# Narrow attention scores in one pass over packed query parts, packed narrow outputs, and two sets of probabilities

## The reference

```python
# wide (layers 0, 2)
q, k, v = hidden @ Wq, ctx @ Wk, ctx @ Wv            # 16 heads of 64
logits = einsum('bhqd,bhkd->bhqk', q, k) * 64**-0.5 + col_bias
out = softmax(logits) @ v ;  out = out @ Wo + bo + residual
# narrow (layers 1, 3)
xn = rmsnorm(x, norm_w); q = xn @ wq                  # 16 heads of 16
k, v = cond @ wk, cond @ wv                           # 4 heads of 16
scores = einsum('btgrd,bsgd->bgrts', qg, k) * 0.25
out = softmax(scores) @ v ;  return residual + out @ wo
```

## Time and profile before

| | us |
|---|---|
| median of 3 runs | 1891.38 |
| lowest, highest | 1888.63, 1896.26 |
| profiled execution | 1886.37 |
| its span on the core | 1883.9 |
| TensorE busy | 1703.7 (90%) |
| VectorE busy | 1251.6 (66%) |
| ScalarE busy | 1040.1 (55%) |
| GpSimd busy | 428.8 (23%) |

### The profile page before, as it was taken

One profiled execution on the slowest core, in us unless ns is written; L12 is line 12 of the kernel. 1 busy time (PEld: TensorE's weight loads), 2 busy tenths in 40 slices (PEclk: granted clock), 3 DMA queues, 4 the chain that ended last, 5 costly groups with the idle time before them and its releaser, 6 DMA issues. The chain is left out here.

```text
span 1883.9 us, 29965 instructions
## 1 busy us (share of the span) xinstructions
PE 1703.7 (90%) x10924; PEld 935.7 (50%) x10924; DVE 1251.6 (66%) x2393; ACT 1040.1 (55%) x1761; POOL 428.8 (23%) x299
## 2 busy tenths in 40 slices
PE   6897597989999999999899999899999999999574
PEld 5786333444545454545445454445454545454333
DVE  4447554667867786878566777577777777776342
ACT  1111063666666666666566666566666666666231
POOL 4242302121222122212111322121212121312201
PEclk9998698999999999999999999999999999999786
DMA  8976542051215121513243324222332233221205
GB/s 270 326 266 207 130 125 47 13 102 35 75 44 124 35 75 44 124 36 95 69 100 76 88 49 101 58 70 60 83 65 71 60 82 66 70 60 50 56 25 201
DMA packets 176025, 175.78 MB, mean 93 GB/s; under 512 B 89538, under 2 KB 131902, under 8 KB 174281
## 3 DMA queue, kind: packets, MB, share of 16 engines
q1 hardware_dynamic: 173576, 163.39, 33.0%
q10 hardware_dynamic: 2304, 10.49, 1.4%
HBM read 127.17 MB, written 46.63 MB: 92 GB/s over the span
## 5 line engine op out<-in xcount | busy, mean ns | idle before, releaser
L1183 DVE TENSOR_REDUCE tops<-general 128x2 bf16<-128x308 f32 x1024 | 436.6, 472 | 105.3 <-PE general L1290 47.8
L1143 POOL TENSOR_TENSOR kept<-kept,inv_b 128x512 f32<-128x512 f32 x192 | 258.6, 1368 | 659.6 <-DMA inv_b<-scratch_inverses 655.3
L1046 ACT ACTIVATE probs<-score_ps 128x512 f32<-128x512 f32 x512 | 299.4, 597 | 137.9 <-PE score_ps L1326 130.4
L1170 DVE CAST q_aux<-q_pair 64x512 bf16<-64x512 f32 x160 | 82.7, 517 | 211.4 <-ACT q_pair L1034 210.3
L1056 ACT ACTIVATE q_aux<-general 4x512 bf16<-4x512 bf16 x320 | 187.6, 586 | 13.6 <-PE general L1297 6.7
L1033 ACT ACTIVATE q_pair<-general 64x512 fp32r<-64x512 f32 x160 | 94.6, 592 | 178.3 <-PE general L1271 178.0
L1082 ACT ACTIVATE a_hi<-kept 128x512 fp32r<-128x512 f32 x192 | 109.9, 621 | 122.3 <-POOL kept L1143 62.8
L1196 DVE TENSOR_TENSOR a_lo<-kept,a_hi 128x512 fp32r<-128x512 f32 x192 | 149.8, 821 | 28.6 <-ACT a_hi L1082 27.8
L1216 DVE TENSOR_TENSOR x<-general,x 128x512 f32<-128x512 f32 x160 | 108.4, 690 | 80.5 <-PE general L1384 79.2
L1286 PE MATMUL general<-w_top,q_aux 128*128 128x154 bf16 x1024 | 125.7, 234 | 24.0 <-DVE q_pair L1173 10.5
L1131 POOL TENSOR_TENSOR x_lo<-xn,x_hi 128x1024 fp32r<-128x1024 f32 x32 | 75.8, 2368 | 308.0 <-ACT x_hi L1014 157.1
(11 more groups left out here) (150 smaller groups left out, 3249.3 us busy)
## 6 DMA issues: line engine op xcount, KB each, us to landing
inv_b<-scratch_inverses SPq DMA_DIRECT2D x128, 256.0 KB
inv_b<-scratch_inverses SPq DMA_DIRECT2D x128, 128.0 KB
xn<-scratch_stream SPq DMA_DIRECT2D x16, 512.0 KB, 3.8
w_pair<-scratch_wk_hi SPq DMA_DIRECT2D x32, 256.0 KB
x<-scratch_stream SPq DMA_DIRECT2D x16, 512.0 KB, 3.3
scratch_stream<-x SPq DMA_DIRECT2D x16, 512.0 KB, 4.0
scratch_wk_hi<-p_kout_hi SPq DMA_DIRECT2D x16, 308.0 KB
p_raw<-in_L_xattn_Wk_dram SPq DMA_DIRECT2D x4, 1024.0 KB, 6.9
```

Source lines behind the costliest of these rows:

```text
L1046: nc.scalar.activation(dst, score_ps[:, number % 2, :], ACT.Exp, scale=scale).then_inc(act_exp.sem, 1)
L1143: last = nc.gpsimd.tensor_tensor(tile, tile, inv_b[:, i, :], ALU.mult)
L1183: last = nc.vector.tensor_reduce(tops[:, n % 2, sub, 2 * pair:2 * pair + 2], src, AX_X, ALU.max)
```

## The change

- **Narrow scores in one pass.** `q_pair` for narrow steps holds tiles of 32 rows (two heads of 16) in three bands: high part, low part, high part again, and four rows (96 to 99) of negated maxima. The keys `n_pair` lie against them as high, high, low keys, and ones for the maxima, all in fp32r. So a narrow score is one matmul, not two; `n_aux` is gone. A narrow `rest` is two fp32r matmuls over pairs of heads, where it was one fp32r and one bf16.
- To fill the bands: DVE casts the whole query bank to bf16 (`n_query`, for the maxima), ACT makes four copies of 32 rows, DVE four subtractions of 32 rows, POOL copies the high band (32 x 2048) to rows 64 to 95. A narrow `turn` writes two tiles instead of one.
- **Packed narrow outputs.** Values of odd key heads are laid in the other 16 rows of each 32. Two tiles are scaled by inverses that are zero on the rows of sums (`inv_n`, 16-row DMAs, eight a batch where four were) and POOL adds them into one. `norm`, `low` and `output` of a narrow batch then handle one tile and six matmuls, not two and twelve.
- **Two probability sets.** `probs` is doubled; the exponential waits for `value` two steps back.
- Inverses have one DRAM buffer and one spread buffer for each kind of layer, so `inverse c` waits for the scales of the chunk two back, not the one before. The `general` banks are counted over the whole plan. `ORDER` is a new one.

```diff
-        sums=d("sums", (H, TOK), F32), inverses=d("inverses", (H, TOK), F32),
+        sums=d("sums", (H, TOK), F32), inverses=d("inverses", (2, H, TOK), F32),
...
+        n_query = sb("n_query", [P, 2, TOK], BF16)
-        probs = sb("probs", [P, 4, TOK])
+        probs = sb("probs", [P, 2, 4, TOK])
...
# SP, inverses of a narrow chunk
+                        for j in range(4):
+                            at = 32 * j + DN * h
+                            src = rows[4 * j + 2 * batch + h:4 * j + 2 * batch + h + 1]
+                            sp.dma_start(inv_n[at:at + DN, h, :], src.to_broadcast([DN, TOK])).then_inc(inv_loaded[1].sem, 16)
...
# ACT
+                        wait(act, dve_aux.sem, dve_aux.after(it, what, n, k))
+                        for pair in range(4):
+                            last = nc.scalar.activation(q_pair[0:32, s, pair, :], ps[32 * pair:32 * pair + 32], ACT.Copy)
...
-                    before_w, before = back_step(it, n, 3 if what == "rest" else 1)
+                    before_w, before = back_step(it, n, 3 if what == "rest" else 2)
...
+                        for pair in range(2):
+                            last = nc.scalar.activation(q_pair[96:100, slot(n), 2 * (n % 2) + pair, :], tops_t, ACT.Copy, scale=-1.0)
...
-                    for i in range(2):
+                    for i in range(1 + (n + 1) % 2):
                         tile = chunk_tile(n, 2 * k + i)
                         last = nc.scalar.activation(a_hi[:, i, :], kept[:, place(tile), :], ACT.Copy)
...
# POOL
+                    wait(pool, act_query.sem, act_query.after(it, what, n, k))
+                    pool.wait_ge(*latest)
+                    q = q_pair[:, slot(n)]
+                    nc.gpsimd.tensor_copy(q[64:96], q[0:32]).then_inc(pool_query.sem, 1)
...
+                    if n % 2:
+                        last.then_inc(pool_parts.sem, 1)
+                        wait(pool, pool_parts.sem, pool_parts.after(it, "scale", n, k))
+                        last = nc.gpsimd.tensor_tensor(tiles[0], tiles[0], tiles[1], ALU.add)
...
# DVE
+                        wait(dve, pe_query.sem, pe_query.after(it, what, n, k))
+                        nc.vector.tensor_copy(n_query[:, s, :], ps).then_inc(dve_aux.sem, 1)
...
+                        for pair in range(4):
+                            last = nc.vector.tensor_tensor(q_pair[32:64, s, pair, :], ps[32 * pair:32 * pair + 32], q_pair[0:32, s, pair, :], ALU.subtract)
...
# PE
+                        if not wide(n):
+                            wait(pe, pool_query.sem, pool_query.after(it, *query_for(n, 1)))
...
-                        h, unit = 4 * g + k, k if wide(n) else n % 2
-                        if what == "rest":
-                            keys = (n_pair_rest[:, g], n_aux_rest[:, g])
-                        else:
-                            keys = (w_pair[:, h], w_aux[:, h]) if wide(n) else (n_pair[:, h], n_aux[:, h])
-                        nc.tensor.matmul(ps, keys[0], q_pair[:, s, unit, :], start=True, stop=False)
-                        last = nc.tensor.matmul(ps, keys[1], q_aux[:, t, s, unit, :], start=False, stop=True)
+                        last = nc.tensor.matmul(ps, n_pair[:, 4 * g + k], q_pair[:, s, 2 * (n % 2) + k // 2, :], start=True, stop=True)
...
-                        pairs = [q for i in range(2) for q in split3(w[0][:, 2 * k + i, rows], w[1][:, 2 * k + i, rows], a_hi[:, i, :], a_lo[:, i, :])]
+                        tiles = [(2 * k + i, i) for i in range(2)] if n % 2 == 0 else [(k, 0)]
+                        pairs = [q for at, i in tiles for q in split3(w[0][:, at, rows], w[1][:, at, rows], a_hi[:, i, :], a_lo[:, i, :])]
```

Of the new `ORDER`, the narrow steps 4 to 6, which the inverses and scales of chunk 0 run through:

```diff
+    rest 4, score 4 0, score 4 1, max 5 6, max 5 7, score 4 2, max 6 0, max 6 1, score 4 3, turn 5,
+        max 6 2, max 6 3, inverse 0, split 2, value 4 1, max 6 4, max 6 5,
+    rest 5, score 5 0, max 6 6, output 3- 1, score 5 1, max 6 7, score 5 2, max 7 0, max 7 1, score 5 3,
+        query 8 0, turn 6, value 5 1,
+    rest 6, max 7 2, max 7 3, score 6 0, scale 0 0, norm 0 0, max 7 4, max 7 5, scale 0 1, max 7 6,
+        scale 0 2, max 7 7, max 8 0, score 6 1, max 8 1, score 6 2, scale 0 3, max 8 2, turn 7, max 8 3,
+        score 6 3, low 0 0, query 8 1,
```

More of the change, by code:

```diff
@@ L558 @@
-    rest 15, value 14 1, score 15 0, output 2 0, wkeys 0+ 2, score 15 1, max 0+ 4, wkeys 0+ 3, score 15 2,
-        norm 2 1, max 0+ 5, max 0+ 6, score 15 3, max 0+ 7, low 2 1, query 1+ 0, turn 0+, value 15 1,
-        scale 2 2, output 2 1, norm 2 2, scale 2 3, max 1+ 0, low 2 2, query 1+ 1
+    rest 0, max 1 0, score 0 0, max 1 1, max 1 2, score 0 1, sums 3-, max 1 3, score 0 2, max 1 4,
+        max 1 5, value 0 0, scale 2- 2, max 1 6, norm 2- 2, score 0 3, scale 2- 3, inverse 3-, max 1 7,
+        scale 3- 0, low 2- 2, query 2 0, turn 1, value 0 1, output 2- 2, max 2 0, norm 2- 3,
@@ new lines @@
+    rest 10, max 11 0, max 11 1, max 11 2, value 9 0, max 11 3, scale 1 0, max 11 4, score 10 0, max 11 5,
+        score 10 1, max 11 6, max 11 7, score 10 2, score 10 3, turn 11, value 9 1, query 12 0, early 0+,
+    rest 11, max 12 0, value 10 0, scale 1 1, max 12 1, norm 1 0, score 11 0, value 10 1, max 12 2,
+        score 11 1, max 12 3, max 12 4, score 11 2, max 12 5, low 1 0, max 12 6, score 11 3, max 12 7,
+        query 14 0, turn 12, value 11 0, value 11 1, max 13 0, max 13 1, sums 2, max 13 2,
@@ new lines @@
+    rest 12, max 13 3, max 13 4, score 12 0, max 13 5, max 13 6, score 12 1, max 13 7, score 12 2,
+        output 1 0, turn 13, inverse 2, score 12 3, norm 1 1, max 14 0, max 14 1, max 14 2, max 14 3,
+    rest 13, split 0+, max 14 4, wkeys 0+ 0, max 14 5, score 13 0, low 1 1, max 14 6, score 13 1, max 14 7,
+        value 12 1, max 15 0, max 15 1, score 13 2, max 15 2, turn 14, output 1 1, score 13 3, max 15 3,
+    rest 14, max 15 4, scale 2 0, max 15 5, wkeys 0+ 1, score 14 0, norm 2 0, max 15 6, max 15 7,
+        score 14 1, low 2 0, query 0+ 0, wkeys 0+ 2, turn 15, query 0+ 1, wkeys 0+ 3, score 14 2,
+        value 13 1, score 14 3, output 2 0,
@@ L561 @@
+    rest 15, scale 2 1, max 0+ 0, score 15 0, max 0+ 1, max 0+ 2, score 15 1, norm 2 1, max 0+ 3, max 0+ 4,
+        value 14 1, max 0+ 5, max 0+ 6, score 15 2, max 0+ 7, low 2 1, score 15 3, query 1+ 0, turn 0+,
+        query 1+ 1, value 15 1, output 2 1
 """
@@ L575, in window @@
     return order
-WINDOW = window()
-ROUNDS = range(-1, ITER + 1)
+WINDOW = window(ORDER)
 def chunk_of(what, n):
@@ L620, in back_tile, with plan @@
     return w, tile
+def plan():
+    entries = []
+    for r in range(-1, ITER + 1):
+        entries += [(r + turn, what, n, k) for what, n, k, turn in WINDOW if present(r + turn, what, n)]
+    return entries
+PLAN = plan()
 class Signal:
```

302 lines of the change are left out of this document (145 added, 157 removed).

## The result

| | before | after |
|---|---|---|
| median | 1891.01 us (20 runs, 1885.62 to 1897.32) | 1899.08 us (20 runs, 1890.10 to 1907.92) |
| ratio, 95% interval | | 1.0041 (1.0025 to 1.0058) |
| span of the profiled execution | 1883.9 us | 1903.0 us |

The forecast was 1811 us; the change makes the kernel slower by 0.4%, some 8 us. The profiled execution of after took 1904.78 us, 5.7 above its median, so its spans overstate the loss.

A forecast was written before the change was run, and what follows sets the result against it. TensorE's work was taken as the bound. Scores -56, rest +2, outputs -45, probabilities -4, new waits +20 and edges +3 gave -80 us: 1806 from the profiled 1886.4, 1811 as median, range 1788 to 1860.

The forecast's parts named there:

- TensorE's own work sets the time, and what leaves its queue leaves the total.: Whole kernel: TensorE, busy 185.8 of 188.6 us in a steady window, was the bound until another engine is level.
- Narrow scores -56, rest +2, narrow outputs -45: TensorE's queue: 256 score and 192 output matmuls go, 64 rest matmuls change kind; about 99 us less in all.
- VectorE +6, ScalarE +55, "covered": Added work in us over the run on these two engines, claimed to lie beside TensorE's work and cost no time.
- GpSimd's copy 3.2 us, addition 1.37: Times of GpSimd's 32 x 2048 query copy and its narrow output addition, 32 each; GpSimd was to stay mostly idle.
- Inverses level: Narrow norms were to come about level with their scales, where the old order left 4 to 11 us.
- Two sets of probabilities -4: The second set removes the narrow scores' wait for value of the step before: -4 us (0 to -10).
- New waits +20 (0 to +64): Longer-held general banks of narrow queries and two tight norms make TensorE wait 2.5 us in each of 8 windows.
- Edges +3: Start and end of the run, as chains around the last narrow output and first narrow keys: +3 us (-6 to +8).
- A, the narrow chunks become VectorE's: Rival: TensorE and VectorE come level in narrow chunks, which don't shrink, so only some 48 us are gained: 1843 us, 17%.
- B, the weight load: Rival: the removed score matmul also hid the next one's weight load, 0.11 us for each of 256: 1839 us, 8%.
- C, the shared port: Rival: GpSimd's long copies hold VectorE through the SBUF port they share, 2 us each, 32 times: 1855 us, 8%.
- D, rest waits for the copy behind a scale: Rival: narrow rest waits for GpSimd's copy, queued behind a scale; TensorE loses 4 us a query: 1919 us, slower, 5%.

The follow-up runs named there:

- e6: The kernel before with both low products of every narrow output left out, 256 matmuls fewer: 1886.06 us, ratio 0.9977.
- e3: The kernel before with two sets of probabilities and nothing else: 1890.62 us, ratio 1.0012.
- f1: The changed kernel with a signal for each of ScalarE's four narrow query copies, so VectorE's first subtraction starts behind the first copy: 1864.41 us, ratio 0.9872.
- e5: The changed kernel with the narrow query's low parts cut to 64 of 512 columns and their keys left at zero: 1867.52 us, ratio 0.9885.
- e1: The changed kernel with the ORDER of the kernel before: 1932.93 us, ratio 1.0220.
- f2: f1 with the wide queries' two copies signalled one by one as well: 1830.01 us, ratio 0.9687 against the kernel before.
- f5: f2 with the ORDER of the kernel before: 1898.10 us, ratio 1.0044 against the kernel before.

## Why the prediction was wrong, step by step

**"TensorE's own work sets the time, and what leaves its queue leaves the total."** This is the step that failed. 185.8 busy of 188.6 us was read as a cause. It was an outcome: matmuls and the releases they wait for had come out level, so TensorE seemed never to wait. e6 shows it without any of the change: -60 us of matmuls, -5 us of time. The Trainium skill (Perfetto Trace Analysis, "Identifying the Most-Contended Engine") says to optimize the engine of highest occupancy first, but excepts TensorE, since a matmul's busy share is no good measure of how near it is to its limit, and goes by the share of its peak that is useful work and by its weight loads' busy share. This case bears out the exception: in the window the matmuls are 98% busy, the weight loads 51% (95.8 of 188.6 us), and the engine gave back a twelfth of what was taken from it.

**Narrow scores -56, rest +2, narrow outputs -45.** As work, right. The sums of start distances in window 2, before and after (32 scores of each kind and 24 outputs' worth of matmuls left), fell by 6.7 us for the second score matmul, 5.6 for the outputs and rose by 0.3 for the rest: 12.0 a window, for 12.4 forecast. My own sums over those starts; the counts are the page's 10924 to 10476. The distance behind a narrow score's start rose from 0.33 to 0.46 us, but that is mean wait (the 12.8 us of idle time before these scores, and waits of the maxima behind them); the middle one of the distances is 0.34, as before.

**VectorE +6, ScalarE +55, "covered".** The amounts held: +7.3 and +41.1 us on the page. "Covered" did not. They are not beside the path, they are links in it: query, ScalarE, VectorE, bank. A busy share says nothing of that.

**GpSimd's copy 3.2 us, addition 1.37.** It is 1.886 us (x32) and 1.302. The copy was taken near the two-input operation of the earlier trace rows; it came out at the memset beside it. It did no harm, and no wait on it stands in TensorE's groups.

**Inverses level.** Held in the main: ScalarE's `norm` waits for scales 32.7 + 24.0 us, for 62.8, and TensorE's wait for `a_lo` in front of narrow outputs is 28.1 for 19.4, in front of wide ones 9.5 for 6.1. Some 12 us more; part of the two tight norms that the forecast counted.

**Two sets of probabilities -4.** Nothing (e3). With two sets e3 still waits 5.9 us for `probs`, for 7.6 with one, and TensorE after the change waits 12.5 us for `probs_rest`: ScalarE is late, not the buffer.

**New waits +20 (0 to +64).** The mis-sized term. From what was to be saved, 12.0 x 8 = 96 us, and the 8 us that were lost, it is about +100 in all. On the pages 63 us of it are idle time of TensorE; the rest is busy time, which fell by 43.8 us where 96 us of starts went. The length of the hold was worked out rightly as 5.8 us; measured, 852.12 to 858.12 = 6.0. The slack was not. I counted banks, and charged only what exceeds two uses, 1.3 us twice a window, as if all else of the hold were free. f1 and e5 price it: 35 us for 32 x 1.8 us of hold and 32 us for 32 x 1.9, so 0.5 to 0.6 us for each us. A narrow query of before held its bank for 3.5 us (median, from ScalarE's first copy to the last subtraction), so 2.5 us more for each of 32 is some 40 to 48 us, an estimate from these two prices. That is twice the term, and not half of what came. The cause of the rest of the 100 us stays open: the trace shows the 25 us of new waits behind wide queries, 12 more for `a_lo`, and the lower clock.

**The clock, not in the forecast.** The kernels in which TensorE has fewer matmuls or more waits show more time at the low granted clock. In window 2 of after, behind a short wait at 626.54 and sixteen matmuls of one column, the twelve matmuls of a query start 0.43 us apart at first, then 0.23 again (timeline of TensorE; the earlier trace rows has 0.23 at the high level):

```profile
627.62 1.95 PE L1432 MATMUL general<-ones,xn 128*128 128x1 f32 x16
...
630.16 0.63 PE L1308 MATMUL general<-x_lo,wq_hi 128*128 128x512 f32 x1
630.59 0.63 PE L1308 MATMUL general<-x_hi,wq_lo 128*128 128x512 f32 x1
...
633.03 0.39 PE L1308 MATMUL general<-x_hi,wq_lo 128*128 128x512 f32 x1
633.26 0.40 PE L1308 MATMUL general<-x_hi,wq_hi 128*128 128x512 f32 x1
```

That is 1.2 GHz for 2.4: the granted clock from 629.40 to 632.90 is 0.51. The stretch from 400 to 1700 us, before first, after second (columns as in the earlier trace rows):

```profile
400.00:1700.00 1300.00, 1264.13 (x8467) 652.57 (x8466) 959.25 (x1802) 849.74 (x1462) 296.27 (x203) 0.99 0.30 71
```

```profile
400.00:1700.00 1300.00, 1210.72 (x7964) 611.68 (x7956) 957.59 (x1780) 871.69 (x1522) 372.80 (x252) 0.98 0.30 66
```

The clock is 0.99 in before, 0.98 in after and e6, 0.97 in e1: one hundredth of 1300 us is 13 us of TensorE's work. So part of a matmul taken out can be paid back in slower ones. Over whole executions the mean granted clock has these medians: 0.952 in before, 0.942 in e6, 0.941 in after, 0.948 in f1, 0.949 in f2, 0.935 in f5, 0.932 in e1. One hundredth of 1890 us is 19 us at full speed (an estimate of TensorE's work, not of the kernel's time). By it the clock takes about as much from e6 as the new waits do, and some 21 us from after; and of the 35 and 69 us that f1 and f2 win, 13 and 15 could come through the clock. It need not be a cause apart, since after, f1 and f2 run the same matmuls and differ in their waits alone; no run here separates the two.

**Edges +3.** From the first `rest` of the last chunk to the end it is 92.4 us for 83.8, so +8.6, with f1 and e5 at 88.3 and 88.8; the first step of the first window came 5.2 us earlier (240.0 for 245.2). The sum, +3.4, is as forecast.

**The rivals.** *A, the narrow chunks become VectorE's:* nearest in kind, since it spoke of coupled engines, but chunk 3 is at 36.1 us and chunk 1, which it expected to stay, grew; and no engine is full there. It failed on where. *B, the weight load:* the mean distance reached 0.46, but through waits; a narrow score is followed at 0.34 in the median, as its first matmul was before. No. *C, the shared port:* the longest `a_lo` is 1861 ns for 1800, and the excess over 686 ns, (843 - 686) x 160 = 25 us, is not more than before's (821 - 686) x 192 = 26. No. *D, rest waits for the copy behind a scale:* GpSimd's copy waited 10.5 us for inverses, in 2 of 32 cases, and TensorE never for it. No. D was the one slower case, and the time came out on its side by another mechanism: one engine standing inside the query while three queues are behind it. Even that holds for a part of it only, some 45 us by the prices above. That mechanism was in the text as a cost of 2.5 us a window. That the time fell on the slower side is not to D's credit: its own wait, of `rest` for GpSimd's copy, never happened.

**What would show it.** The prediction was to be wrong "if idle time in the narrow chunks passes 5 us a window". It is 5.54 + 1.43 = 7.0 in window 2, and the second sign named, waits put to the query's subtractions and `a_lo`, is where it stands.

**Two slips of arithmetic.** The low end of the range is said to be all gains at their bound with 5 us of waits; that is -104 - 10 + 5 - 6 = -115, so 1776 us, not 1788. And D, at 5%, is split into 4% slower and 2% same. Neither bears on what failed.

## What to carry to other kernels

An engine that is 98% busy under an order written by hand may still not be the bound; before counting on a removed instruction, follow what releases the first wait behind it, and ask how much that release would have to move as well. When a change puts more operations of two engines on one PSUM bank in turn, price by how much longer the bank is held (here 0.5 to 0.6 us for each us, also where two other banks seemed to leave slack), and signal each piece, so that the second engine starts behind the first piece: here that alone, at the narrow and the wide queries, turned +8 us into -61. Look for the new waits behind the steps that were not changed, too: more of them stood there. And parts can look worthless or harmful alone and pay together: the new parts in the old order cost 42 us, the finer signals in the old kernel gave 8, and with the new order the two give 61.

## What the runs showed of the hardware

- ScalarE can copy one band of 32 rows of a PSUM bank while VectorE subtracts from another band of the same bank, at no cost: in f2, where 96 of the 128 subtractions overlap such a copy, they have 679/685/695 ns (minimum, median, maximum), as in after where they never overlapped. The Trainium skill (PSUM — Partial Sum Buffer, "PSUM bank collisions raise a hardware error") says that different quadrants of one bank may be accessed at the same time; f1 and f2 agree. By the same section of the Trainium skill two engines in one quadrant at a time are an error, which the cast of all 128 rows beside a copy would be; no run here tried it.
- GpSimd's fp32 copy of 32 x 2048 takes 1.886 us, 0.92 ns a column, level with a memset of as many columns (1.804) and 0.41 of a two-input operation (4.566). An addition of 512 columns takes 1.302.
- ScalarE's copies of 4, 32 and 64 rows take 577, 589 and 591 ns at 512 columns: cutting a tile by rows multiplies the time. VectorE's subtraction from PSUM the same, 685 for 32 rows and 684 for 64.
- VectorE's cast to bf16 takes 692 ns from PSUM (128 rows) and 419 to 424 from SBUF (64 rows), medians in after.
